# Third feed-forward of a four-layer kernel: expert outputs stored by plain indirect DMA to a table of two rows per token, both tables read back and added to x

## The chip, the cores and the metric

One core of one Trainium2 chip runs the kernel. The metric is device time in microseconds. The kernel before was run three times: 4308.01, 4302.86 and 4307.19 us, median 4307.19.

## The reference

`x` holds 64 sequences of 128 tokens of width 128. Four layers follow, each a cross attention to `ctx` and a feed-forward; every one adds to `x`. The third feed-forward, where nearly all of the change lies, is a mixture of experts with capacity: 8 experts with 512 hidden units, two experts per token, at most 2048 tokens per expert. Cut to what matters:

```python
h = layernorm(x)                                  # 8192 tokens of width 128
first, second = two best experts of softmax(h @ wg)
slot = number of earlier choices of that expert   # all first choices, then all second ones
weight = gate where slot < 2048, else 0           # a choice over capacity is dropped
y[e] = gelu(rows[e] @ w1[e] + b1[e]) @ w2[e] + b2[e]
x = x + weight_1 * y[first, slot_1] + weight_2 * y[second, slot_2]
```

The first feed-forward (another kind of expert layer, "proto") is touched as well, because tables in DRAM are filled there ahead of time.

## The kernel before

`x` stays in SBUF in 64 blocks of 128 tokens, one token per partition. The program is a row of phases; each ends in a barrier of all engines, so no phase starts before the one before it has ended on every engine.

The third feed-forward is `dispatched_experts_phase`. The routing ahead of it gives each token's two choices a row number in the DRAM table `dispatched` (8 experts x 2048 rows, 130 floats each: 128 of the normalized token, its weight, and an integer that says where the output goes). A choice that is dropped gets a spare row behind the table. The phase then has three parts.

1. The scatter. GpSimd (POOL) issues 2 x 64 indirect DMAs (L1935), one for each choice and block of 128 tokens. The weight column of `X.rows` is written by VectorE (DVE) between the two passes, once the first pass has landed (L1996, L1998). The integer column holds the token's number and is written once (L1928). SyncE (SP) meanwhile stores all of `x` to the DRAM table `summed` (L1961).
2. The tiles. The table is worked off in 32 tiles of 512 rows, four tiles per expert, in an order written out by hand for each engine. For tile t: SP loads it into `XR[t % 4]` (L1958) after the output stores of tile t-4 have landed, since these read the same buffer's indices; PE transposes it (`rows_turn`, L2060) into `f_px`, which it does for tile t+1 right behind the first unit of tile t; four hidden units of 128 follow, each with three passes up (`f_pu`) and three passes down (`f_py`), the down passes two units behind; DVE and ScalarE (ACT) split operands and apply gelu (L2022, L1981, L1985); ACT adds the bias (`f_ys`, L2028), PE transposes back (`f_po`, L2088) behind the last unit of the next tile, ACT scales by the weight into `YO[t % 2]` (L2035), and POOL issues four indirect DMAs of 128 rows that add into `summed` (L1945, `compute_op=ALU.add`). ACT writes `YO` only when the stores of tile t-2 have landed. At each fourth tile POOL waits for the landing of the four tiles before, so that two experts never add to the same row at once.
3. The return. When all stores have landed, SP loads `summed` back into `x` in eight parts of 512 KB (L1968), and DVE takes the statistics of each block for the next layernorm (L2008).

Rows of `dispatched` that no token takes must be harmless: in the first feed-forward POOL clears a tile `f_empty` (L1332), writes numbers of spare rows into its integer column (L1334), and SP stores it eight times over the table (L1323). POOL's first copies of the gates, `f_gs` (L1340), stand behind these; PE's first matmul (`f_pt`, L1470) waits for these copies and for a split of the bias by DVE (L1375, L1377).

Of the kernel before, what the change touches and what calls it, by code (L numbers as in the profile page):

```python
# [13 lines left out]
F32 = mybir.dt.float32  # L14
# [3 lines left out]
I32 = mybir.dt.int32  # L18
ALU = mybir.AluOpType
# [3 lines left out]
P = 128  # L23
# [1229 lines left out]
def gated_rows_phase(nc, R, I, name, kind):  # L1253
# [14 lines left out]
    with ExitStack() as stack:  # L1268
# [34 lines left out]
        func = ACT.Copy if kind == "proto" else ACT.Gelu  # L1303
        GBL = BL - UNG
        if kind == "proto":
            empty = sb(n_("empty"), [P, 16, ROW])
            empty_ready, table_empty = sem(n_("empty_ready")), sem(n_("table_empty"))

        def lagged(g, c, par, first, lag, f):

# [5 lines left out]
        with nc.Block() as block:  # L1316
            if kind == "proto":
                @block.sync
                def _(sp):
                    sp.wait_ge(empty_ready, 2)  # L1320
                    table = R.dispatched[0:E2 * CAP, :].rearrange("(i p r) w -> i p r w", p=P, r=16)
                    for i in range(E2 * CAP // (16 * P)):
                        sp.dma_start(table[i], empty[:]).then_inc(table_empty, 16)  # L1323
                    sp.wait_ge(table_empty, 16 * (E2 * CAP // (16 * P)))

            @block.gpsimd
            def _(pool):
                pool.wait_ge(Z["split"], 5)
                if TERMS > 3:
                    pool.wait_ge(Z["zeroed"], 1)  # L1330
                if kind == "proto":
                    nc.gpsimd.memset(empty[:], 0.0).then_inc(empty_ready, 1)  # L1332
                    pool.wait_ge(empty_ready, 1)
                    nc.gpsimd.iota(empty[:].bitcast(I32)[:, :, D + 1], [[1, 16]], base=NB * P,  # L1334
                                   channel_multiplier=16).then_inc(empty_ready, 1)

                def stage(g, par):
                    at_least(pool, Z["gt_psum"], g - 1)
                    src = g3[:, bass.ds(g * GB, GB), :, :].rearrange("p b t e -> p b (t e)")
# [529 lines left out]
def dispatched_experts_phase(nc, R, I, name):  # L1869
# [12 lines left out]
    with ExitStack() as stack:  # L1882
# [24 lines left out]
        PX = [ps(n_(f"px{i}"), [P, TR]) for i in range(2)]  # L1907
        PO = [ps(n_(f"po{i}"), [P, 4, D]) for i in range(2)]
        spare_ready, index, placed = sem(n_("spare_ready")), sem(n_("index")), sem(n_("placed"))
        ids_ready, weighted, x_kept = sem(n_("ids_ready")), sem(n_("weighted")), sem(n_("x_kept"))  # L1910
        xr_in, x_in = [sem(n_(f"xr_in{i}")) for i in range(4)], [sem(n_(f"x_in{i}")) for i in range(PARTS)]
        Z = {s: sem(n_(s)) for s in ("px_ready", "xh_ready", "xl_ready", "up_ready", "a_ready", "hi_ready", "lo_ready",
                                     "dn_ready", "ys_ready", "po_ready", "yo_ready")}
        tile_of = lambda rows, t: rows[t * TR:(t + 1) * TR, :].rearrange("(p r) d -> p r d", r=4)

        def adds(t):

            return 64 * (t // 4 + 1)

# [4 lines left out]
        with nc.Block() as block:  # L1924
            @block.gpsimd
            def _(pool):
                nc.gpsimd.iota(spare_i[:], [[NB * P, 2], [P, NB]], base=E * CAP, channel_multiplier=1).then_inc(spare_ready, 1)
                nc.gpsimd.iota(X.rows[:].bitcast(I32)[:, :, D + 1], [[P, NB]], base=0,  # L1928
                               channel_multiplier=1).then_inc(ids_ready, 1)
                pool.wait_ge(ids_ready, 1)  # L1930
                pool.wait_ge(placed, 1)
                for i in range(2):
                    pool.wait_ge(weighted, i + 1)
                    for b in range(NB):
                        nc.gpsimd.indirect_dma_start(  # L1935
                            out=R.dispatched[:, :], out_offset=bass.IndirectOffsetOnAxis(ap=place[:, i, b:b + 1], axis=0),
                            in_=X.rows[:, b, :], in_offset=None).then_inc(R.scattered, 16)
                pool.wait_ge(x_kept, 16 * PARTS)
                for t in range(NT):
                    pool.wait_ge(Z["yo_ready"], t + 1)  # L1940
                    if t % (NT // E) == 0:
                        for before in range(max(0, t - 4), t):
                            pool.wait_ge(R.added[before % 4], adds(before))
                    for j in range(4):
                        nc.gpsimd.indirect_dma_start(  # L1945
                            out=R.summed[:, :],
                            out_offset=bass.IndirectOffsetOnAxis(ap=XR[t % 4][:].bitcast(I32)[:, j, D + 1:D + 2], axis=0),
                            in_=YO[t % 2][:, j, :], in_offset=None, compute_op=ALU.add).then_inc(R.added[t % 4], 16)

            @block.sync  # L1950
            def _(sp):
                view = R.summed[0:NB * P, :].rearrange("(b t) d -> t b d", t=P)
                part = lambda i: slice(i * NB // PARTS, (i + 1) * NB // PARTS)

                def load(t):
                    if t >= 4:
                        sp.wait_ge(R.added[t % 4], adds(t - 4))
                    sp.dma_start(XR[t % 4][:], tile_of(R.dispatched, t)).then_inc(xr_in[t % 4], 16)  # L1958

                for i in range(PARTS):  # L1960
                    sp.dma_start(view[:, part(i), :], R.x[:, part(i), :]).then_inc(x_kept, 16)  # L1961
                sp.wait_ge(R.scattered, 16 * 2 * NB)
                for t in range(NT):
                    load(t)
                for t in range(NT - 4, NT):
                    sp.wait_ge(R.added[t % 4], adds(t))
                for i in range(PARTS):
                    sp.dma_start(R.x[:, part(i), :], view[:, part(i), :]).then_inc(x_in[i], 16)  # L1968

            @block.vector  # L1970
            def _(dve):
                v = nc.vector

                def split_low(t):
                    dve.wait_ge(Z["xh_ready"], t + 1)
                    v.tensor_tensor(XL[t % 2][:], PX[t % 2][:], XH[t % 2][:].bitcast(F32), ALU.subtract).then_inc(Z["xl_ready"], 1)

                def high(n):
# [12 lines left out]
                v.tensor_tensor(X.kept[:], X.kept[:], spare[:], ALU.mult).then_inc(index, 1)  # L1991
                v.tensor_tensor(spare[:], spare[:], X.slots[:], ALU.add).then_inc(index, 1)
                dve.wait_ge(index, 3)
                v.tensor_tensor(place[:], spare[:], X.kept[:], ALU.subtract).then_inc(placed, 1)
                dve.wait_ge(ids_ready, 1)
                v.tensor_copy(X.rows[:, :, D], X.weight[:, 0, :]).then_inc(weighted, 1)  # L1996
                dve.wait_ge(R.scattered, 16 * NB)
                v.tensor_copy(X.rows[:, :, D], X.weight[:, 1, :]).then_inc(weighted, 1)  # L1998
                split_low(0)
                for n in range(N):  # L2000
                    high(n)
                    low(n)
                    if n % HB == 2 and n // HB + 1 < NT:
                        split_low(n // HB + 1)
                for b in range(NB):
                    if b % (NB // PARTS) == 0:
                        dve.wait_ge(x_in[b // (NB // PARTS)], 16)
                    v.bn_stats(R.stats[:, b, :], R.x[:, b, :]).then_inc(R.stats_done, 1)  # L2008

            @block.scalar  # L2010
            def _(act):
# [18 lines left out]
                def outs(t):  # L2030
                    act.wait_ge(Z["po_ready"], t + 1)
                    if t >= 2:
                        act.wait_ge(R.added[(t - 2) % 4], adds(t - 2))
                    for j in range(4):
                        last = a.activation(YO[t % 2][:, j, :], PO[t % 2][:, j, :], ACT.Identity,  # L2035
                                            scale=XR[t % 4][:, j, D:D + 1])
# [69 lines left out]
def build(nc, I, out):  # L2106
    with ExitStack() as stack:
# [7 lines left out]
        R.ones_bf = sb("ones_bf", [P, P], BF16)  # L2115
        R.stats_done = sem("stats_done")
        R.dispatched = nc.dram_tensor("dispatched", [E2 * CAP + 2 * NB * P, ROW], F32).ap()
        R.summed = nc.dram_tensor("summed", [NB * P + SPARE, D], F32).ap()
        R.scattered = sem("scattered")
        R.added = [sem(f"added{i}") for i in range(4)]  # L2120
# [109 lines left out]
```

## Time and profile before

| | us |
|---|---|
| median of three runs | 4307.19 |
| lowest and highest | 4302.86, 4308.01 |
| the profiled execution | 4304.42 |
| its span from first to last instruction | 4302.6 |
| third feed-forward: from the first scatter to the end of the last statistics | 1996.6 to 2538.5 |
| of it the tiles, first load to last store | 2164.2 to 2518.4 |

The profile comes from one execution. Its durations are that execution's; PE is the matmul stream, PEld the weight loads beside it. An engine that issues a DMA is busy only as long as the issue takes; POOL's indirect DMAs are work of POOL, because it makes the descriptors. `A <- B` behind a wait says which instruction ended it, as far as the profile can tell. The column PEclk in the table by stretches is the granted TensorE clock as a share of 2.4 GHz.

### The profile page before, as it was taken

What the parts mean: (1) busy time and instruction counts of PE and PEld (TensorE: products, weight loads), DVE (VectorE), ACT (ScalarE), POOL (GpSimd) and SP (SyncE); (2) the same over time, 40 slices, a digit from 0 to 9 for tenths busy, and PEclk for the clock granted to TensorE, in tenths of its full rate; (3) what the DMA queues carried; (4) which work ended last, traced back from release to release, by engine and by line L of the source; (5) the groups of instructions that cost most, each with busy time, mean ns of one, the idle gap of its engine ahead of it and who ended that gap; (6) DMA issues with size and microseconds to landing.
All of it is one profiled execution on the core that took longest, in us unless ns stands there. A gap on an engine that the chain in (4) does not pass through costs nothing. (4 is left out here: it accounts for less than half of the span.)

```text
span 4302.6 us, 95379 instructions
## 1 busy us (share of the span) xinstructions
PE 3552.4 (83%) x31830; PEld 2474.5 (58%) x31831; DVE 3327.7 (77%) x6125; ACT 2333.0 (54%) x4244; POOL 1642.7 (38%) x909
## 2 busy tenths in 40 slices
PE   6983979999598899982067749999499998799999
PEld 3552646667365566662045536666366666677777
DVE  7888879997897888883044458888788778788888
ACT  3432657775475566640044436767566665466665
POOL 2210045552000545433745555555155443222222
PEclk9985989997799999985588869999699999799999
DMA  1012022222000222212123342222222112100000
GB/s 62 16 35 96 0 63 63 66 63 68 1 0 11 66 56 59 56 62 61 51 48 50 50 89 60 60 59 57 58 54 53 46 46 67 40 15 15 15 15 15
DMA packets 172168, 200.65 MB, mean 47 GB/s; under 512 B 37692, under 2 KB 126080, under 8 KB 169793
## 3 DMA queue, kind: packets, MB, share of 16 engines
q1 hardware_dynamic: 149441, 181.01, 15.7%
q0 software_dynamic: 22528, 16.92, 2.9%
q8 instruction: 132, 2.16, 0.2%
q14 instruction: 67, 0.55, 0.0%
HBM read 48.90 MB, written 38.01 MB: 20 GB/s over the span
## 5 line engine op out<-in xcount | busy, mean ns | idle before, releaser
L704 ACT ACTIVATE a_p<-a_p 128x480 f32<-128x480 f32 x832 | 501.6, 603 | 517.4 <-DVE a_p L552 515.1
L348 POOL TENSOR_TENSOR a_km<-a_k,a_slots 96x1920 fp32r<-96x1920 f32 x186 | 631.8, 3417 | 179.9 <-DMA a_k<-a_kh 179.9
L547 DVE TENSOR_REDUCE a_mx<-a_sc 128x4 f32<-128x480 f32 (+1 forms) x832 | 542.2, 652 | 126.2 <-PE a_sc L792 96.5
L552 DVE TENSOR_TENSOR a_p<-a_sc,a_mx 128x480 f32<-128x480 f32 x832 | 531.2, 638 | 18.8
L710 ACT ACTIVATE a_pt<-a_tp 120x512 f32<-120x512 f32 x832 | 487.8, 586 | 82.9 <-PE a_tp L801 77.8
L801 PE MATMUL a_tp<-ident,a_p 128*120 128x128 f32 x3328 | 510.0, 276 | 4.1 <-ACT a_p L704 2.3
L801 PEld LDWEIGHTS a_tp<-ident,a_p 128*120 128x120 f32 x3328 | 400.0, 138 | 90.0 <-ACT a_p L704 27.1
L786 PE MATMUL a_sc<-a_km,a_qr 96*128 96x480 f32 x768 | 395.8, 515 | 33.6 <-DMA a_qr<-a_ql 29.5
L825 PE MATMUL a_nd<-a_pt,a_vm 120*32 120x128 f32 x6656 | 354.5, 285 | 0.0
L825 PE MATMUL a_nd<-a_pt,a_dm 120*32 120x128 f32 x6656 | 334.4, 273 | 0.0
L1760 ACT ACTIVATE f_s<-f_pu 128x512 f32<-128x512 f32 x256 | 153.5, 600 | 212.8 <-PE f_pv L1249 212.8
L1945 POOL DMA_INDIRECT summed<-f_yo,f_xr x128 | 202.5, 1582 | 153.2 <-ACT f_yo L2035 118.8
L547 DVE TENSOR_REDUCE s_mx<-s_sc 128x4 f32<-128x512 f32 x256 | 176.3, 689 | 97.4 <-PE s_sc L792 96.7
L2060 PE MATMUL f_px<-ident,f_xr 128*128 128x128 f32 x128 | 27.4, 353 | 271.5 <-DMA f_xr<-dispatched 271.5
L560 DVE RECIPROCAL a_rd<-a_nd 128x128 f32<-128x128 f32 x256 | 242.4, 947 | 6.7 <-PE a_nd L825 6.5
L348 POOL TENSOR_TENSOR s_km<-s_k,s_slots 96x2048 fp32r<-96x2048 f32 x62 | 224.0, 3633 | 52.2 <-DMA s_k<-s_kh 52.2
L1646 POOL TENSOR_TENSOR f_ya<-f_ya,f_yg 128x512 f32<-128x512 f32 x96 | 125.1, 1303 | 302.4 <-DVE f_yg L1696 302.3
L704 ACT ACTIVATE s_p<-s_p 128x512 f32<-128x512 f32 x256 | 161.1, 629 | 146.1 <-DVE s_p L552 144.6
L1671 DVE TENSOR_TENSOR f_a<-f_s,f_pv 128x512 f32<-128x512 f32 x256 | 175.2, 684 | 76.5 <-ACT f_s L1760 68.7
L1683 DVE TENSOR_TENSOR f_al<-f_a,f_ah 128x512 fp32r<-128x512 f32 x256 | 229.0, 895 | 0.0
L786 PEld LDWEIGHTS a_sc<-a_km,a_qr 96*128 96x128 f32 x768 | 146.4, 191 | 138.3 <-issue 130.1
L825 PEld LDWEIGHTS a_nd<-a_pt,a_vm 120*32 120x32 f32 x6656 | 131.2, 108 | 141.6 <-issue 132.2
(426 smaller groups left out, 8983.4 us busy)
## 6 DMA issues: line engine op xcount, KB each, us to landing
a_qr<-a_qh SPq DMA_DIRECT2D x384, 64.0 KB, 2.0
a_k<-a_kh SPq DMA_DIRECT2D x384, 60.0 KB, 2.0
a_ctx<-in_ctxT SPq DMA_DIRECT2D x64, 240.0 KB, 2.7
a_qr<-a_ql SPq DMA_DIRECT2D x192, 64.0 KB, 2.0
a_k<-a_kl SPq DMA_DIRECT2D x192, 60.0 KB, 2.0
dispatched<-f_empty SPq DMA_DIRECT2D x8, 1040.0 KB, 12.2
f_xr<-dispatched SPq DMA_DIRECT2D x32, 260.0 KB
s_k<-s_kh SPq DMA_DIRECT2D x128, 64.0 KB, 2.0
```

What stands on the lines that cost most here:

```text
L348: v.tensor_tensor(KM[par][:, i, :, :].rearrange("p b (j k) -> p b j k", k=KN), K3[:, i, :, :].unsqueeze(2).to_broadcast([TR, GB, 4, KN]), ...
L547: v.tensor_reduce(mx[:], view, AX.X, ALU.max).then_inc(mx_ready, 1)
L552: v.tensor_tensor(PR[s % 4][:].rearrange("p (h k) -> p h k", k=k), view, mx[:].unsqueeze(2).to_broadcast([P, heads, k]), ALU.subtract).the ...
L560: v.reciprocal(RD[:], ND[bt % 2][:, 1, :]).then_inc(rd_ready, 1)
L704: a.activation(PR[s % 4][:], PR[s % 4][:], ACT.Exp).then_inc(exp_ready, 1)
L710: a.activation(PT[s % 4][0:KN, :], TP[s % 2][0:KN, :], ACT.Copy).then_inc(pt_ready, 1)
L786: last = t.matmul(SC[s % 2][:, 0:W], queries, keys, start=True, stop=not masked)
L801: last = t.transpose(TP[s % 2][0:KN, q * P:(q + 1) * P], PR[s % 4][:, q * KN:(q + 1) * KN], R.ident[:])
L825: last = t.matmul(ND[j % 2][32 * q:32 * q + 32, what, :], w, PT[s % 4][0:KN, q * P:(q + 1) * P], start=(what == 0 and i == 0), stop=(i == ...
L1671: v.tensor_tensor(A[s % 2][:], S[s % 2][:], PV[s % 2][:], ALU.mult).then_inc(Z["a_ready"], 1)
L1683: v.tensor_tensor(AL[s % 4][:], A[s % 2][:], AH[s % 4][:].bitcast(F32), ALU.subtract).then_inc(Z["lo_ready"], 1)
L1945: nc.gpsimd.indirect_dma_start(out=R.summed[:, :], out_offset=bass.IndirectOffsetOnAxis(ap=XR[t % 4][:].bitcast(I32)[:, j, D + 1:D + 2], a ...
```

## The change

The table `summed` (one row per token) becomes `chosen`, with one row per token for its first choice and one for its second, and spare rows behind. The integer column of a dispatched row says which of the two halves, so POOL writes it anew between the two passes of the scatter. No two stores now have the same target row, and they are plain. `x` stays in SBUF and is no longer stored; at the end SP loads both halves part by part into two buffers `YB`, and DVE adds them to `x`, taking the statistics of the part before in between. POOL's wait at each fourth tile goes. Since rows of dropped choices are never written, `chosen` is filled with zeros in the first feed-forward: a second memset on POOL ahead of the one of `f_empty`, and eight more stores of 1 MB on SP. The semaphores `added` are renamed `returned`.

```diff
@@ first feed-forward @@
                 def _(sp):
+                    sp.wait_ge(none_ready, 1)
+                    chosen = R.chosen[0:2 * NB * P, :].rearrange("(i p r) d -> i p (r d)", p=P, r=16)
+                    for i in range(2 * NB // 16):
+                        sp.dma_start(chosen[i], none[:]).then_inc(chosen_zero, 16)
                     sp.wait_ge(empty_ready, 2)
...
+                    sp.wait_ge(chosen_zero, 16 * (2 * NB // 16))
...
+                    nc.gpsimd.memset(none[:], 0.0).then_inc(none_ready, 1)
                     nc.gpsimd.memset(empty[:], 0.0).then_inc(empty_ready, 1)
                     pool.wait_ge(empty_ready, 1)
-                    nc.gpsimd.iota(empty[:].bitcast(I32)[:, :, D + 1], [[1, 16]], base=NB * P,
+                    nc.gpsimd.iota(empty[:].bitcast(I32)[:, :, D + 1], [[1, 16]], base=2 * NB * P,
@@ third feed-forward, POOL @@
-                nc.gpsimd.iota(X.rows[:].bitcast(I32)[:, :, D + 1], [[P, NB]], base=0,
-                               channel_multiplier=1).then_inc(ids_ready, 1)
-                pool.wait_ge(ids_ready, 1)
                 pool.wait_ge(placed, 1)
                 for i in range(2):
+                    at_least(pool, R.scattered, 16 * NB * i)
+                    nc.gpsimd.iota(X.rows[:].bitcast(I32)[:, :, D + 1], [[P, NB]], base=i * NB * P,
+                                   channel_multiplier=1).then_inc(ids_ready, 1)
+                    pool.wait_ge(ids_ready, i + 1)
                     pool.wait_ge(weighted, i + 1)
...
-                pool.wait_ge(x_kept, 16 * PARTS)
                 for t in range(NT):
                     pool.wait_ge(Z["yo_ready"], t + 1)
-                    if t % (NT // E) == 0:
-                        for before in range(max(0, t - 4), t):
-                            pool.wait_ge(R.added[before % 4], adds(before))
                     for j in range(4):
                         nc.gpsimd.indirect_dma_start(
-                            out=R.summed[:, :],
+                            out=R.chosen[:, :],
...
-                            in_=YO[t % 2][:, j, :], in_offset=None, compute_op=ALU.add).then_inc(R.added[t % 4], 16)
+                            in_=YO[t % 2][:, j, :], in_offset=None).then_inc(R.returned[t % 4], 16)
@@ third feed-forward, SP @@
-                for i in range(PARTS):
-                    sp.dma_start(view[:, part(i), :], R.x[:, part(i), :]).then_inc(x_kept, 16)
...
                 for i in range(PARTS):
-                    sp.dma_start(R.x[:, part(i), :], view[:, part(i), :]).then_inc(x_in[i], 16)
+                    at_least(sp, x_added, i - 1)
+                    for k in range(2):
+                        sp.dma_start(YB[i % 2][:, k, :, :], choice[k][:, part(i), :]).then_inc(y_in[i % 2], 16)
@@ third feed-forward, DVE @@
-                for b in range(NB):
-                    if b % (NB // PARTS) == 0:
-                        dve.wait_ge(x_in[b // (NB // PARTS)], 16)
-                    v.bn_stats(R.stats[:, b, :], R.x[:, b, :]).then_inc(R.stats_done, 1)
+                def statistics(i):
+                    dve.wait_ge(x_added, i + 1)
+                    for b in range(i * NB // PARTS, (i + 1) * NB // PARTS):
+                        v.bn_stats(R.stats[:, b, :], R.x[:, b, :]).then_inc(R.stats_done, 1)
+
+                for i in range(PARTS):
+                    dve.wait_ge(y_in[i % 2], 32 * (i // 2 + 1))
+                    x = R.x[:, part(i), :]
+                    v.tensor_tensor(x, x, YB[i % 2][:, 0, :, :], ALU.add).then_inc(first_added, 1)
+                    dve.wait_ge(first_added, i + 1)
+                    v.tensor_tensor(x, x, YB[i % 2][:, 1, :, :], ALU.add).then_inc(x_added, 1)
+                    if i > 0:
+                        statistics(i - 1)
+                statistics(PARTS - 1)
```

## Rows read from the trace of the kernel before

**Rows 1.** The page, part 1: busy us, share of the span, instructions.

```profile
PE 3552.4 (83%) x31830; PEld 2474.5 (58%) x31831; DVE 3327.7 (77%) x6125; ACT 2333.0 (54%) x4244; POOL 1642.7 (38%) x909
```

**Rows 2.** Waits, 2164 to 2560: who for whom: us, times, longest.

```profile
PE f_px L2060 <- DMA f_xr<-dispatched: 271.5, 15, 191.5
...
POOL summed L1945 <- ACT f_yo L2035: 118.8, 15, 25.0
```

**Rows 3.** Stretch, tile 4 to 30: length; PE, PEld, DVE, ACT, POOL busy; PEclk; DMA, GB/s.

```profile
2199.90:2479.03 279.13, 202.21 (x833) 157.31 (x833) 130.53 (x234) 126.93 (x260) 164.25 (x105) 0.84 0.37 50
```

**Rows 4.** Timeline of one turn: start, duration, instruction, [idle before <- releaser].

```profile
2328.59 1.12 PE L2060 MATMUL f_px<-ident,f_xr 128*128 128x128 f32 x4 [5.56 <-DMA f_xr<-dispatched]
...
2336.61 1.14 ACT L2035 ACTIVATE f_yo<-f_po,f_xr 128x128 f32<-128x128 f32 x4 [0.45 <-PE f_po L2088]
...
2338.03 1.56 POOL L1945 DMA_INDIRECT summed<-f_yo,f_xr  x1 [6.63 <-ACT f_yo L2035]
...
2343.78 1.56 POOL L1945 DMA_INDIRECT summed<-f_yo,f_xr  x1 [0.30 <-issue]
...
2347.11 0.32 SPq L1958 DMA_DIRECT2D f_xr<-dispatched  x1
...
2350.13 1.11 PE L2060 MATMUL f_px<-ident,f_xr 128*128 128x128 f32 x4 [5.67 <-DMA f_xr<-dispatched]
```

**Rows 5.** Groups on POOL, scatter and tiles: count, busy us, mean ns, idle before.

```profile
L1935 POOL DMA_INDIRECT dispatched<-f_rows,f_place x128 | 122.9, 960 | 45.2 <-issue 43.2 <-DVE f_rows L1996 2.0
...
L1945 POOL DMA_INDIRECT summed<-f_yo,f_xr x128 | 202.5, 1582 | 153.2 <-ACT f_yo L2035 118.8 <-issue 34.1 <-DMA summed<-f_yo,f_xr 0.3
```

**Rows 6.** Timeline of the scatter: ends of its two passes, first tile's load.

```profile
2071.32 0.96 POOL L1935 DMA_INDIRECT dispatched<-f_rows,f_place  x1 [0.30 <-issue]
...
2076.37 0.95 POOL L1935 DMA_INDIRECT dispatched<-f_rows,f_place  x1 [0.30 <-issue]
...
2161.67 0.95 POOL L1935 DMA_INDIRECT dispatched<-f_rows,f_place  x1 [0.30 <-issue]
2164.19 1.90 SPq L1958 DMA_DIRECT2D f_xr<-dispatched  x4
```

**Rows 7.** Stretch behind a stall (columns as rows 3), and PE's timeline behind two others.

```profile
2328.60:2332.90 4.30, 4.30 (x12) 3.56 (x13) 0.00 (x0) 0.59 (x2) 2.50 (x2) 0.50 0.42 39
...
3201.16 0.79 PE L786 MATMUL s_sc<-s_km,s_qr 96*128 96x512 f32 x1 [3.34 <-issue]
...
2176.01 0.50 PE L1245 MATMUL f_pu<-f_xh,f_w1hi 128*128 128x512 f32 x1 [1.59 <-ACT f_a L2022]
```

**Rows 8.** Timeline of the last outputs and the return; time to landing of its loads.

```profile
2500.16 1.14 ACT L2035 ACTIVATE f_yo<-f_po,f_xr 128x128 f32<-128x128 f32 x4 [0.44 <-PE f_po L2088]
...
2505.22 1.14 ACT L2035 ACTIVATE f_yo<-f_po,f_xr 128x128 f32<-128x128 f32 x4 [2.97 <-DMA summed<-f_yo,f_xr]
...
2516.82 1.55 POOL L1945 DMA_INDIRECT summed<-f_yo,f_xr  x1 [0.30 <-issue]
...
2520.19 11.16 SPq L1968 DMA_DIRECT2D x<-summed  x8
...
2524.33 1.64 DVE L2008 BATCH_NORM_STATS2 stats<-x 128x6 f32<-128x128 f32 x8 [23.42 <-DMA x<-summed]
...
2535.17 3.31 DVE L2008 BATCH_NORM_STATS2 stats<-x 128x6 f32<-128x128 f32 x16 [0.16 <-DMA x<-summed]
...
DMA to landing us min/median/max: 4.1/7.2/7.8
```

**Rows 9.** Timeline of the first feed-forward's start.

```profile
394.90 2.29 DVE L1365 TENSOR_TENSOR f_rest<-f_gates,f_g 128x2048 f32<-128x2048 f32 x1
...
402.10 1.84 POOL L1332 MEMSET f_empty<- 128x2080 f32 x1 [85.97 <-DVE f_g L1371]
...
402.53 1.49 DVE L1375 CAST f_bias<-f_bias 96x128 bf16<-96x128 f32 x1
...
405.35 0.66 PE L1470 MATMUL f_pt<-ident_bf,f_gs 128*96 128x128 bf16 x4 [67.01 <-DVE f_bias L1377]
```

More of the change, by code:

```diff
@@ L1305, in gated_rows_phase @@
         if kind == "proto":
-            empty = sb(n_("empty"), [P, 16, ROW])
+            empty, none = sb(n_("empty"), [P, 16, ROW]), sb(n_("none"), [P, 16 * D])
             empty_ready, table_empty = sem(n_("empty_ready")), sem(n_("table_empty"))
+            none_ready, chosen_zero = sem(n_("none_ready")), sem(n_("chosen_zero"))
         def lagged(g, c, par, first, lag, f):
@@ L1909, in dispatched_experts_phase @@
         spare_ready, index, placed = sem(n_("spare_ready")), sem(n_("index")), sem(n_("placed"))
-        ids_ready, weighted, x_kept = sem(n_("ids_ready")), sem(n_("weighted")), sem(n_("x_kept"))
-        xr_in, x_in = [sem(n_(f"xr_in{i}")) for i in range(4)], [sem(n_(f"x_in{i}")) for i in range(PARTS)]
+        YB = [sb(n_(f"yb{i}"), [P, 2, NB // PARTS, D]) for i in range(2)]
+        ids_ready, weighted = sem(n_("ids_ready")), sem(n_("weighted"))
+        first_added, x_added = sem(n_("first_added")), sem(n_("x_added"))
+        xr_in, y_in = [sem(n_(f"xr_in{i}")) for i in range(4)], [sem(n_(f"y_in{i}")) for i in range(2)]
         Z = {s: sem(n_(s)) for s in ("px_ready", "xh_ready", "xl_ready", "up_ready", "a_ready", "hi_ready", "lo_ready",
@@ L1914, in dispatched_experts_phase, with part, rows_back @@
         tile_of = lambda rows, t: rows[t * TR:(t + 1) * TR, :].rearrange("(p r) d -> p r d", r=4)
-        def adds(t):
+        def part(i):
+            return slice(i * NB // PARTS, (i + 1) * NB // PARTS)
+        def rows_back(t):
             return 64 * (t // 4 + 1)
@@ L1937, in _ @@
                             in_=X.rows[:, b, :], in_offset=None).then_inc(R.scattered, 16)
-                pool.wait_ge(x_kept, 16 * PARTS)
                 for t in range(NT):
                     pool.wait_ge(Z["yo_ready"], t + 1)
-                    if t % (NT // E) == 0:
-                        for before in range(max(0, t - 4), t):
-                            pool.wait_ge(R.added[before % 4], adds(before))
                     for j in range(4):
                         nc.gpsimd.indirect_dma_start(
-                            out=R.summed[:, :],
+                            out=R.chosen[:, :],
                             out_offset=bass.IndirectOffsetOnAxis(ap=XR[t % 4][:].bitcast(I32)[:, j, D + 1:D + 2], axis=0),
-                            in_=YO[t % 2][:, j, :], in_offset=None, compute_op=ALU.add).then_inc(R.added[t % 4], 16)
+                            in_=YO[t % 2][:, j, :], in_offset=None).then_inc(R.returned[t % 4], 16)
             @block.sync
             def _(sp):
-                view = R.summed[0:NB * P, :].rearrange("(b t) d -> t b d", t=P)
-                part = lambda i: slice(i * NB // PARTS, (i + 1) * NB // PARTS)
+                choice = [R.chosen[k * NB * P:(k + 1) * NB * P, :].rearrange("(b t) d -> t b d", t=P) for k in range(2)]
                 def load(t):
                     if t >= 4:
-                        sp.wait_ge(R.added[t % 4], adds(t - 4))
+                        sp.wait_ge(R.returned[t % 4], rows_back(t - 4))
                     sp.dma_start(XR[t % 4][:], tile_of(R.dispatched, t)).then_inc(xr_in[t % 4], 16)
-                for i in range(PARTS):
-                    sp.dma_start(view[:, part(i), :], R.x[:, part(i), :]).then_inc(x_kept, 16)
                 sp.wait_ge(R.scattered, 16 * 2 * NB)
@@ L1965, in _ @@
                 for t in range(NT - 4, NT):
-                    sp.wait_ge(R.added[t % 4], adds(t))
+                    sp.wait_ge(R.returned[t % 4], rows_back(t))
                 for i in range(PARTS):
-                    sp.dma_start(R.x[:, part(i), :], view[:, part(i), :]).then_inc(x_in[i], 16)
+                    at_least(sp, x_added, i - 1)
+                    for k in range(2):
+                        sp.dma_start(YB[i % 2][:, k, :, :], choice[k][:, part(i), :]).then_inc(y_in[i % 2], 16)
             @block.vector
@@ L1994, in _ @@
                 v.tensor_tensor(place[:], spare[:], X.kept[:], ALU.subtract).then_inc(placed, 1)
-                dve.wait_ge(ids_ready, 1)
                 v.tensor_copy(X.rows[:, :, D], X.weight[:, 0, :]).then_inc(weighted, 1)
@@ L2032, in outs @@
                     if t >= 2:
-                        act.wait_ge(R.added[(t - 2) % 4], adds(t - 2))
+                        act.wait_ge(R.returned[(t - 2) % 4], rows_back(t - 2))
                     for j in range(4):
@@ L2117, in build @@
         R.dispatched = nc.dram_tensor("dispatched", [E2 * CAP + 2 * NB * P, ROW], F32).ap()
-        R.summed = nc.dram_tensor("summed", [NB * P + SPARE, D], F32).ap()
+        R.chosen = nc.dram_tensor("chosen", [2 * NB * P + SPARE, D], F32).ap()
         R.scattered = sem("scattered")
-        R.added = [sem(f"added{i}") for i in range(4)]
+        R.returned = [sem(f"returned{i}") for i in range(4)]
         load_phase(nc, R, I)
```

## The prediction

> **What bounds the kernel now.** I read three things in order. First the page: PE is busy for 83% of the span and POOL for 38% [rows 1], so a change on POOL counts only where POOL is what the others wait for. Then the waits of the third feed-forward, 2164 to 2560 us. There PE's largest wait is for a load of dispatched rows, and POOL's largest is for ACT's scaled outputs [rows 2]. The first wait is 271.5 us in 15 pieces, but one piece of 191.5 us is the routing and the scatter ahead of the tiles; the other 14 are 80 us, 5.7 us each. PE waits for a load, the load waits for POOL's adding stores, and POOL waits for outputs that PE has not made: a loop. Third, the timeline of one turn of this loop [rows 4].
>
> The loop runs like this. PE turns the rows of tile t+4 early in tile t+3. Its buffer XR is that of tile t, so the load waits until tile t's four stores have landed. From tile 16's turn at 2328.59, PE, DVE and ACT need 9.16 us until ACT has finished tile 14's outputs at 2337.75. POOL starts 0.28 later and spends 7.31 on four adding stores, 2338.03 to 2345.34. 1.77 us later, at 2347.11, SP issues tile 18's load. 3.02 later PE starts it at 2350.13. The sum is 9.16 + 0.28 + 7.31 + 1.77 + 3.02 = 21.54 us, which is the whole distance 2328.59 to 2350.13. It covers two tiles: tile 15's stores run behind tile 14's, and the next odd load is in time. PE's last matmul of the turn ends at 2344.46, so PE is idle for 5.67 of the 21.54. Over 13 turns, 279.13 us [rows 3], a turn takes 21.47. So nothing here is PE-bound; the loop is latency, and POOL's four stores are a third of it.
>
> **The stores: removed and added.** One adding indirect DMA holds POOL 1.58 us on average, a plain one of the dispatch 0.96, both 128 of 128 rows [rows 5]. With the gap between instructions a plain one comes every 1.26 us (2071.32 to 2076.37 are four steps [rows 6]), so four take 3 x 1.26 + 0.95 = 4.73 in place of 7.31. The trace has no plain store of 512-byte rows from YO with indices in XR; its nearest row is the dispatch, with 520-byte rows and indices in another tile, and I take it. Bounds: 4.73 as above, 7.31 if the 1.58 is not due to the adding. From the last plain issue to what waits for its landing the trace has 2161.67 + 0.95 = 2162.62 to 2164.19, so 1.57 [rows 6], against 1.77 for the adding one. Saved per turn: 2.58 + 0.20 = 2.78. There are 14 stalls of PE, and each turn keeps a stall (5.67 - 2.78 = 2.9), so the loop still sets the pace and all of it counts: 14 x 2.78 = 38.9 us.
>
> What is late next in a turn: tile 19's load. Its tile 15 outputs are made 6.8 us after tile 14's, its stores then take 4.73 + 1.57 + 3.02 behind them, 0.3 us of waiting included about 16.4 us after tile 14's outputs; PE wants it 9.6 us after them to restart on tile 18 and some 8.4 later, so 18.0. It is in time by 1.6 us. POOL's own load falls from 15 to 10 us per turn of 18.8.
>
> The landing time was weighed against a rule. The Trainium skill, Perfetto Trace Analysis, in its account of the lifecycle of a DMA, says that the semaphore update waits until the write is confirmed and that this can take surprisingly long when the target is HBM. That speaks against any gain from a plain store, which still writes HBM; the row agrees in that 1.57 us remain. By the rule alone the landing would gain nothing, 36.1 in place of 38.9.
>
> **The clock.** After a stall of 5.56 us the granted clock is 0.50 (1.2 GHz) for 4.3 us of matmuls, then 1.00 (2.4 GHz) [rows 7]. The 4.3 us would be half as long at the upper level, so each fall costs 2.15 us, inside the 9.16. With a stall of 2.9 us it may not fall. The nearest rows: behind a stall of 3.34 us the first matmul of 512 columns took 0.79, the lower level (all six stalls of 3.3 to 3.7 us ended so), behind one of 1.59 it took 0.50, the upper one [rows 7] (of 13 stalls near 1.5 us, 3 were followed by a fall within 3 us). 2.9 is nearer to the former. I take 10 falls in 14, so 4 x 2.15 = 8.6 us gained; bounds 0 and 14 x 2.15 = 30.
>
> **The end of the tiles.** The last 16 stores ran without a break, and the last ended at 2518.37 [rows 8]. ACT's last outputs waited 2.97 us for a landing. With stores of 1.26 us POOL is up to date again after each tile; only the last two tiles, whose outputs come quickly one after the other, still queue: tile 30's outputs end at 2501.30, and eight issues from about 2501.6 end at 2511.4, so 7.0 earlier, and 0.2 for the landing: 7.2 us. Bounds: 2.4 (the last tile's four alone, 4 x 0.6) and 9.8 (16 x 0.61). The removed wait at every fourth tile costs nothing today: it falls where POOL waits for ACT anyway, and this is the cover.
>
> **x comes back: the price.** Before, eight DMAs of 512 KB, issued from 2520.19; the first landed after 4.14, six more follow 1.81 us apart (2524.33 to 2535.17), and the last statistics end at 2538.48 [rows 8]: 18.3 us, set by the transfer. After, 16 such DMAs, at most two parts (four DMAs) under way, and two adds of 128 x 1024 per part on DVE. An add over 2048 columns took 2.29 [rows 9], so one over 1024 takes about 1.22, if a fixed 0.15 is in it; two and their link 2.5. Eight statistics take 1.64. I followed the parts one by one: parts 0 and 1 land 5.9 and 9.5 us after the first issue. Part 2's loads go out when part 0 is added (8.5), part 3's when part 1 is (12.1), and so on; two loads need 2.2 + 2 x 1.8 us when the queue has run dry. DVE adds (2.5), then takes the statistics of the part before (1.6). This gives a part every 4.2 to 4.3 us, DVE and the round through SP nearly equal; part 7 is added at 38.4, and 16 statistics end at 41.7. That is 23.4 more than 18.3; with some slack at SP I take 24. From below: transfer alone, 2.3 + 16 x 1.81 + 2.5 + 3.3 = 37.1, so 18.8 more. From above: each pair of parts pays the median landing of 7.2 [rows 8], a second DMA's 1.8, the adds' 2.5 and 0.3: 11.8 for two parts, 47 + 3.3 = 50.5, so 32 more.
>
> **The start of the stage.** The eight stores of x to the old table vanish; they lay beside the scatter, whose pace does not depend on them, so nothing is gained. POOL now writes the ids after waiting for placed, and a second time after the first pass has landed: two short iotas of 64 columns with a semaphore each, 0.3 us each and 0.6 together. Behind each wait the scatter's issues are queued, and for them SP's loads and PE. From above each costs no more than the 2080-column memset, 1.84 [rows 9].
>
> **The first feed-forward.** POOL gets a second memset, 2048 columns, ahead of the old one, which took 1.84, and its first copies of the gates stand behind both. During it a DVE cast in the chain of the bias took 1.49, while PE stood waiting for this chain (405.35) [rows 9]. So the start of PE moves by one memset less what slack there is: 1.9 us, bounds 0 and 3.7. The 8 MB of zeros go out beside matmuls, on an SP that has nothing else in that stage, which lasts until about 600 us; cover is ample, and without it they would cost about 20 us.
>
> **Sum.** -38.9 - 8.6 - 7.2 + 24 + 0.6 + 1.9 = -28.2 us. The profiled execution took 4304.42 us (span 4302.6 and 1.8 around it), so 4276.2; it lies 2.8 below the median of the runs, 4307.19, and the forecast on that footing is 4279.
>
> **Rivals.** *The clock stays up.* If 2.9 us are short enough at all 14 turns, 30 us are gained in place of 8.6, and the time is 4258. For it: 10 of 13 stalls near 1.5 us left the clock alone. Against: all six of 3.3 to 3.7 brought it down. Chance 0.22. The Trainium skill, TensorE: Matmul & The Clock Gate, section on HAM oscillation, describes this pattern, a DMA wait per tile that makes every tile start cold, and would have it vanish once waits are short.
>
> *The return is latency.* Every pair of parts pays the upper bound: +32 in place of +24, and few turns keep the clock. Then -38.9 - 3 - 7.2 + 32 + 2.5 = -14.6, 4293. For it: two buffers only, and SP, DVE and queue hand over in a circle. Against: the queue holds four DMAs, not one. Chance 0.15.
>
> *Slower: the plain store holds POOL as long as the adding one.* Then the loop keeps its 21.5 us, and only the prices stay: +24 + 2.5 less 14 x 0.2, so 4331. The place is POOL's issue in the tile loop; it decides from about 1.2 us per store on: 14 turns of four and some 11 at the end make 67 stores on the path, and 26.5 / 67 = 0.4 below the 1.58. For it: source rows and index stride differ from the dispatch. Against: both index columns lie with one value per partition, and 128 dispatch issues all took 0.96. Chance 0.08.
>
> **Chances and range.** My forecast 0.52, the rivals 0.22, 0.15, 0.08, and 0.03 for something else. The range 4254 to 4300 takes in the first three cases and leaves about 0.15 out. About 0.2%, 8.6 us, is what a measurement of this kernel can tell from no change. Faster by more: the forecast and the clock rival whole and most of the latency rival, 0.86. Within: 0.05. Slower: 0.09.
>
> **What would show it.** In the trace after: plain stores near 0.96 us on POOL; turns of 18.8 us (16.6 where the clock stays at 1.00), with PE's stalls near 2.9; the last store some 55 us earlier relative to the first load; 16 loads back into x, 16 adds of 1.2 us, and 41 to 43 us from the first of these loads to the last statistics; f_pt's first matmul about 1.9 us later. It would be wrong if stores stayed at 1.5 us, if PE's stalls did not shrink, or if a part took 6 us to come back.

## The result and the profile after

The kernel after takes 4260.7 us (median of four runs, 4258.77 to 4265.72), the kernel before 4305.72 in the runs beside it. The ratio is 0.9898, with a 95% interval of 0.988 to 0.9915: 45 us faster. Forecast was 28 us of gain, 4279, with a range of 4254 to 4300. One execution of the kernel before, run beside four of the experiments, took 8560.5 us, twice the time of all others, and is left out of their ratios.

The page, part 1, of the kernel after (as [rows 1]):

```profile
PE 3539.6 (83%) x31830; PEld 2463.6 (58%) x31831; DVE 3346.6 (79%) x6141; ACT 2332.4 (55%) x4244; POOL 1570.1 (37%) x911
```

The waits of the stage (as [rows 2]), the stretch from tile 4's transposes to tile 30's (as [rows 3]), and POOL's stores (as [rows 5]):

```profile
PE f_px L2078 <- DMA f_xr<-dispatched: 226.1, 15, 192.2
...
POOL chosen L1955 <- ACT f_yo L2053: 130.5, 31, 22.2
...
2193.55:2418.76 225.21, 190.48 (x832) 147.25 (x833) 129.94 (x234) 126.95 (x260) 103.69 (x105) 0.93 0.21 62
...
L1955 POOL DMA_INDIRECT chosen<-f_yo,f_xr x128 | 127.7, 998 | 160.3 <-ACT f_yo L2053 130.5 <-issue 29.8
```

PE still waits for the loads 14 times, now 33.9 us in all (226.1 less the 192.2 ahead of the tiles) in place of 80. POOL now waits for ACT at nearly every tile, 31 times, where before it waited at every second: it has become idle in between. 13 turns take 225.21 us, 17.3 each, in place of 21.5. The granted clock of the stretch rose from 0.84 to 0.93.

One turn (as [rows 4]), timeline of the kernel after:

```profile
2295.51 1.12 PE L2078 MATMUL f_px<-ident,f_xr 128*128 128x128 f32 x4 [2.39 <-DMA f_xr<-dispatched]
...
2303.03 1.14 ACT L2053 ACTIVATE f_yo<-f_po,f_xr 128x128 f32<-128x128 f32 x4 [0.45 <-PE f_po L2106]
...
2304.45 0.96 POOL L1955 DMA_INDIRECT chosen<-f_yo,f_xr  x1 [6.06 <-ACT f_yo L2053]
...
2308.37 0.96 POOL L1955 DMA_INDIRECT chosen<-f_yo,f_xr  x1 [0.30 <-issue]
...
2310.61 0.32 SPq L1967 DMA_DIRECT2D f_xr<-dispatched  x1
...
2313.17 0.66 PE L2078 MATMUL f_px<-ident,f_xr 128*128 128x128 f32 x4 [2.29 <-DMA f_xr<-dispatched]
```

The loop is the same, each link shorter: PE's restart to ACT's outputs, 2295.51 to 2304.17, 8.66; POOL starts 0.28 later; four stores 4.88 (2304.45 to 2309.33); landing 1.28; load 2.56. The sum is 17.66, the distance of the two restarts. Means over the 14 turns, from the same timelines of both kernels:

| us per turn | before | after | saved | x 14 | forecast |
|---|---|---|---|---|---|
| PE's restart to ACT's outputs | 9.10 | 8.19 | 0.91 | 12.7 | 8.6 |
| outputs to POOL's start | 0.31 | 0.27 | 0.04 | 0.6 | 0 |
| four stores | 7.33 | 4.91 | 2.42 | 33.9 | 36.1 |
| landing to SP's load | 1.77 | 1.35 | 0.42 | 5.9 | 2.8 |
| load to PE's restart | 3.02 | 2.63 | 0.39 | 5.5 | 0 |

The return, timeline and landing of the kernel after (as [rows 8]):

```profile
2451.92 30.45 SPq L1977 DMA_DIRECT2D f_yb<-chosen  x16
...
2457.95 1.23 DVE L2021 TENSOR_TENSOR x<-x,f_yb 128x1024 f32<-128x1024 f32 x1 [17.89 <-DMA f_yb<-chosen]
2459.20 1.22 DVE L2023 TENSOR_TENSOR x<-x,f_yb 128x1024 f32<-128x1024 f32 x1
...
2466.25 1.22 DVE L2021 TENSOR_TENSOR x<-x,f_yb 128x1024 f32<-128x1024 f32 x1 [0.79 <-DMA f_yb<-chosen]
...
2487.41 1.22 DVE L2021 TENSOR_TENSOR x<-x,f_yb 128x1024 f32<-128x1024 f32 x1
...
2489.81 3.19 DVE L2016 BATCH_NORM_STATS2 stats<-x 128x6 f32<-128x128 f32 x16
...
DMA to landing us min/median/max: 4.0/5.4/7.2
```

From the first load at 2451.92 to the end of the last statistics at 2493.0 are 41.1 us, in place of 18.3: 22.8 more.

The account of the 44.4 us between the two profiled executions (4304.42 and 4260.05): the tiles, first load to last store's end, went from 354.2 to 286.4 (-67.8); last store to first load back -0.4; the return +22.8; the scatter +0.9; PE's first matmul in the first feed-forward +1.45; the stages behind the return +1.1; the rest, -2.4, lies between that matmul and the scatter, in stages that the change doesn't touch.

### The profile page after: what moved, and what is told of

The parts are those of the page before. It is cut to its first block and busy times, and to the rows that moved or that the text cites. A ratio compares the mean times of both kernels' runs of the same rounds, so it can differ in the third digit from the quotient of the medians.

```text
span 4258.2 us, 95393 instructions
## 1 busy us (share of the span) xinstructions
PE 3539.6 (83%) x31830; PEld 2463.6 (58%) x31831; DVE 3346.6 (79%) x6141; ACT 2332.4 (55%) x4244; POOL 1570.1 (37%) x911
## 3 DMA queue, kind: packets, MB, share of 16 engines
q0 software_dynamic: 8192, 16.92, 1.2%
## 5 line engine op out<-in xcount | busy, mean ns | idle before, releaser
L552 DVE TENSOR_TENSOR a_p<-a_sc,a_mx 128x480 f32<-128x480 f32 x832 | 531.4, 639 | 18.8
L2078 PE MATMUL f_px<-ident,f_xr 128*128 128x128 f32 x128 | 25.0, 328 | 226.1 <-DMA f_xr<-dispatched 226.1
L825 PEld LDWEIGHTS a_nd<-a_pt,a_dm 120*32 120x32 f32 x6656 | 199.1, 110 | 0.0
```

The source lines that it names most:

```text
L552: v.tensor_tensor(PR[s % 4][:].rearrange("p (h k) -> p h k", k=k), view, mx[:].unsqueeze(2).to_broadcast([P, heads, k]), ALU.subtract).the ...
L825: last = t.matmul(ND[j % 2][32 * q:32 * q + 32, what, :], w, PT[s % 4][0:KN, q * P:(q + 1) * P], start=(what == 0 and i == 0), stop=(i == ...
```

## The experiments

All are against the kernel after (4260.7) unless said otherwise. The theory is the loop: a turn is the sum of its five links, and a link counts as long as PE stalls.

**e1_add: the adding alone, put back.**

```diff
-                            in_=YO[t % 2][:, j, :], in_offset=None).then_inc(R.returned[t % 4], 16)
+                            in_=YO[t % 2][:, j, :], in_offset=None, compute_op=ALU.add).then_inc(R.returned[t % 4], 16)
```

> The kernel after with one word put back: its stores into the zeroed table add again, so the result is the same. Everything else of the change stays (no wait at each fourth tile, no store of x, two tables read back). Loop theory: the gain comes from what a store costs between tile t's outputs and tile t+4's load. POOL's four stores take 7.3 us again in place of 4.9, the landing 1.8 in place of 1.3 and the load 3.0 in place of 2.6, a turn 21.4 us in place of 17.3, the tiles 354 us from the first load to the last store's end in place of 286; the return stays at 41. Time 4261 + 67 = about 4328, slower than the kernel before by 0.5%. Rival (the removed waits at every fourth tile, or the removed stores of x, brought the gain): turns stay near 17.3 us and the time near 4261.

Measured: 4330.68 us, ratio to the kernel before 1.006 (1.0042 to 1.0078). Stretch of the tiles, and the waits:

```profile
2162.23:2516.16 353.93, 247.92 (x1024) 192.78 (x1024) 160.72 (x288) 157.67 (x321) 203.62 (x128) 0.83 0.36 48
...
PE f_px L2078 <- DMA f_xr<-dispatched: 272.8, 15, 191.8
...
L1955 POOL DMA_INDIRECT chosen<-f_yo,f_xr x128 | 203.6, 1591 | 151.7 <-ACT f_yo L2053 117.3 <-issue 34.4
```

All five links are those of the kernel before again (9.18, 0.27, 7.39, 1.76, 3.07). So the whole gain in the tiles is the adding's, the shorter landing and load and the clock included; what the change does otherwise costs 26 us against the kernel before.

**e6_waits_back: the other waits and stores that the change removed, put back.**

```diff
+                pool.wait_ge(x_kept, 16 * PARTS)
                 for t in range(NT):
                     pool.wait_ge(Z["yo_ready"], t + 1)
+                    if t % (NT // E) == 0:
+                        for before in range(max(0, t - 4), t):
+                            pool.wait_ge(R.returned[before % 4], rows_back(before))
...
+                for i in range(PARTS):
+                    sp.dma_start(kept_rows[:, part(i), :], R.x[:, part(i), :]).then_inc(x_kept, 16)
```

> The kernel after with what the change removed beside the adding put back: the eight stores of x to DRAM ahead of the tiles (into a tensor that nobody reads), POOL's wait for them, and its wait at every fourth tile for the landing of the four before. Theory (these cost nothing, as they lie beside the scatter and where POOL waits for ACT anyway): turns of 17.3 us, time within 3 us of 4261. Rival (they were part of the gain): some 1.3 us of landing at 8 of the tiles and the stores' time beside the scatter, 10 us or more, 4271 and above.

Measured: 4263.31 us, 0.9898 (0.9881 to 0.9914) of the kernel before, the ratio that the kernel after has. The time lies within the 3 us that the theory allowed, and the rival of 10 us is out. The profiled execution was the slowest of the four (4269.45 us, the others 4258.12 to 4264.82): it had 12 falls of the clock in its turns against 9, its turns took 17.9 us, not the 17.3 expected, and its tiles 296.2. Its stalls are not longer (226.0 us with the 191.6 ahead of the tiles), and PE's work at the lower clock level grew from 35.3 to 51.9 us, half of which is 8 of the 10 us. So the difference is mostly the clock's. About 2 us more lie in the first tiles: tile 0's outputs came 22.4 us after the first load, against 20.3 in the kernel after and 22.7 in the kernel before. No run shows why.

```profile
2162.82:2459.06 296.24, 242.30 (x1024) 187.12 (x1024) 160.06 (x288) 157.58 (x321) 126.97 (x128) 0.89 0.19 58
...
PE f_px L2086 <- DMA f_xr<-dispatched: 226.0, 15, 191.6
```

**e2_ring6 and e9_ring5: the loop opened.** Six buffers, then five, for the dispatched rows.

```diff
-        XR = [sb(n_(f"xr{i}"), [P, 4, ROW]) for i in range(4)]
+        XR = [sb(n_(f"xr{i}"), [P, 4, ROW]) for i in range(6)]
...
-                    if t >= 4:
-                        sp.wait_ge(R.returned[t % 4], rows_back(t - 4))
+                    if t >= 6:
+                        sp.wait_ge(R.returned[t % 6], rows_back(t - 6))
```

> The kernel after with six buffers for dispatched rows in place of four. Loop theory: the load of tile t+6 no longer waits for stores that have not landed, PE's 14 stalls (33.9 us) go and with them the falls of the clock; two tiles take what PE, ACT and DVE need, 13.7 us in place of 17.3. Tiles 286 - 13 x 3.6 = about 240 us, time about 4214 to 4218. Rival (another bound, POOL's stores or the loads' bandwidth, lies just behind): a turn of 16 us or more, 4245 or above.

> The kernel after with five buffers for dispatched rows. Loop theory: the demand on a store's landing moves back by one tile, 6.8 us, and the stalls are 2.3 to 2.9 us each, so one more buffer removes them all, as two did: time about 4210, 2 to 7 us of it from the clock. Rival (six buffers gained by more than the stalls, for example by letting the loads run far ahead): less than half of the 51 us, 4235 or above.

Measured: 4209.94 us (0.9786, 0.9768 to 0.9803, of the kernel before) with six, 4208.26 (0.9778, 0.9762 to 0.9794) with five. PE's wait for the loads and a stretch of the tiles, first of six, then of five buffers:

```profile
PE f_px L2078 <- DMA f_xr<-dispatched: 192.1, 1, 192.1
...
2200.00:2380.00 180.00, 176.79 (x844) 140.12 (x843) 132.13 (x238) 128.99 (x265) 104.63 (x107) 1.00 0.26 75
...
PE f_px L2078 <- DMA f_xr<-dispatched: 191.9, 1, 191.9
...
2200.00:2380.00 180.00, 175.84 (x848) 141.02 (x847) 132.84 (x239) 130.65 (x265) 106.43 (x107) 1.00 0.26 77
```

No stall is left but the one ahead of the tiles, the clock stays at its upper level, and PE is busy 98% of the stretch, at 6.8 us per tile. One more buffer is as good as two, as the sizes say: it gives a store one tile more, 6.8 us, and the stalls were 2.2 to 2.9. What is left of the loop after the change is thus worth another 50 us. With six buffers the tiles went from 286.4 to 235.6 us, 50.8 less: 33.9 are the stalls, and PE's work at the lower clock level fell from 35.3 to 6.0 us, half of which is 14.7. So the clock's share is about 15 us, not the 2 to 7 of the expectation; the total of that expectation came out all the same.

**e3_before_ring6 and e8_add_ring6: the same with adding stores.** The first is the kernel before with six buffers; the second is the kernel after with six and this line.

```diff
-                            in_=YO[t % 2][:, j, :], in_offset=None).then_inc(R.returned[t % 6], 16)
+                            in_=YO[t % 2][:, j, :], in_offset=None, compute_op=ALU.add).then_inc(R.returned[t % 6], 16)
```

> The kernel before, adding stores and all, with six buffers in place of four. Loop theory: the loop of PE, POOL and SP opens, and the next bound is POOL: four adding stores take 7.5 us per tile against 6.8 for PE, and at every fourth tile POOL waits some 2 us for landings. Tiles 20 + 32 x 7.5 + 14 = about 270 us in place of 354, time 4306 - 84 = about 4222: the change's plain stores would then be worth next to nothing, since its return costs 23 us more. Rival (the adding stores themselves, by their traffic or their pace on POOL, set the turn): the time stays within 15 us of 4306.

> Six buffers, the table of two rows per token, but the stores add (as in e1_add). Against the kernel after with six buffers it differs in the adding alone, against the kernel before with six in the waits at every fourth tile and in the return. Loop theory: POOL is the bound with 1.67 + 0.3 us per store, 7.9 us per tile, 253 us for 32 tiles, 21 ahead of the first: tiles about 276 us against 235.6 (plain) and 290.0 (adding, with the waits at every fourth tile); time about 4250. So plain stores are worth some 40 us there and the waits some 14. Rival (PE stays the bound at 6.8 us per tile because POOL catches up): within 5 us of 4210.

Measured: 4240.49 us (0.9854, 0.9836 to 0.9871) for the kernel before with six buffers, 4248.27 (0.9871, 0.9854 to 0.9887) for the adding into the new table. The stores of the first, what ACT waits for there, and the stores of the second:

```profile
L1945 POOL DMA_INDIRECT summed<-f_yo,f_xr x128 | 213.7, 1670 | 78.0 <-issue 36.0 <-ACT f_yo L2035 23.1 <-DMA summed<-f_yo,f_xr 19.0
...
ACT f_yo L2035 <- DMA summed<-f_yo,f_xr: 87.2, 26, 5.8
...
L1955 POOL DMA_INDIRECT chosen<-f_yo,f_xr x128 | 212.6, 1661 | 61.2 <-issue 38.7 <-ACT f_yo L2053 22.5
```

The kernel before with six buffers is 64 us faster than with four and 20 faster than the kernel after: the number of buffers alone does more than the change. The bound is then POOL, as expected, but I had it 18 us too fast. A store took 1.67 us, not 1.58, and the waits at every fourth tile, which cost 0.3 us in the kernel before, now cost 19.0: they lost their cover when POOL became the bound. The second kernel was forecast with 1.67 and at 4250 and came to 4248. So with the loop open, the tiles take 290.0 us (adding, with those waits), 272.4 (adding, without) and 235.6 (plain); plain stores are worth 37 us and the waits 18, against 22.8 for the return.

**e5_return4: a finer return.** 16 parts of half the size through four buffers of half the size, in the same memory.

```diff
+    PTS = 16
...
-        YB = [sb(n_(f"yb{i}"), [P, 2, NB // PARTS, D]) for i in range(2)]
+        YB = [sb(n_(f"yb{i}"), [P, 2, NB // PTS, D]) for i in range(4)]
...
-                    at_least(sp, x_added, i - 1)
+                    at_least(sp, x_added, i - 3)
```

> The kernel after with the return in 16 parts of half the size through four buffers of half the size, the same memory. If the 41.1 us of the return are the hand-over with two buffers (a part's loads start only when the part two before is added), it becomes the transfer's: 2.3 + 16 x 1.81 + a smaller last part, about 35 to 37 us, time 4256. Rival (DVE is the bound, 8 x 4.1 us of adds and statistics): 40 to 42 us, time within 1 us of 4261.

Measured: 4259.71 us, 0.9901 (0.9884 to 0.9919) of the kernel before, not told apart from 4260.7. In its trace the return takes 38.2 us in place of 41.1. DVE's timeline:

```profile
2455.13 0.69 DVE L2022 TENSOR_TENSOR x<-x,f_yb 128x512 f32<-128x512 f32 x1 [0.59 <-DMA f_yb<-chosen]
...
2468.45 0.69 DVE L2024 TENSOR_TENSOR x<-x,f_yb 128x512 f32<-128x512 f32 x1
2469.06 0.87 DVE L2017 BATCH_NORM_STATS2 stats<-x 128x6 f32<-128x128 f32 x4
2469.84 0.67 DVE L2022 TENSOR_TENSOR x<-x,f_yb 128x512 f32<-128x512 f32 x1
```

From 2456 on DVE does not wait once: 2.1 us per half part. The first add starts 3.9 us after the first load in place of 6.0, and DVE's waits behind it shrink from 2.8 to 0.6 us; twice as many, shorter instructions give 1.5 of that back. So the hand-over held only some 2 us, the rest is DVE: both theories were half right, and the return never gets down to the transfer.

**e4_early_memset: the memsets moved ahead of the gates' split.**

```diff
+                if kind == "proto":
+                    nc.gpsimd.memset(none[:], 0.0).then_inc(none_ready, 1)
+                    nc.gpsimd.memset(empty[:], 0.0).then_inc(empty_ready, 1)
                 pool.wait_ge(Z["split"], 5)
...
-                    nc.gpsimd.memset(none[:], 0.0).then_inc(none_ready, 1)
-                    nc.gpsimd.memset(empty[:], 0.0).then_inc(empty_ready, 1)
```

> The kernel after with both memsets of the first feed-forward issued by POOL at the start of its phase, where it stands idle for 86 us, in place of behind the split of the gates. Theory (the two memsets delay PE's first matmul there, directly and by slowing DVE's bias splits from 0.4 to 1.5 us each): the casts take 0.2 to 0.4 us again, and the span from DVE's first bias cast to PE's first f_pt matmul falls from 4.7 us (3.25 in the kernel before) to about 1.7. Worth 3 us, time about 4258, within what the runs can tell from 4261. Rival (the 16 MB of fills, not the memsets, hold the phase back): the span stays near 4.7.

Measured: 4264.36 us, 0.9901 (0.9885 to 0.9918): no gain. The stage's start in the kernel after, then in this one, by DVE, POOL and PE:

```profile
392.70 0.43 DVE L1362 CAST f_xh<-f_htall 128x512 fp32r<-128x512 f32 x1 [0.97 <-PEq L69]
...
393.78 1.22 DVE L1370 CAST f_g<-f_gates 128x2048 bf16<-128x2048 f32 x1
...
402.23 1.81 POOL L1338 MEMSET f_none<- 128x2048 f32 x1 [85.96 <-DVE f_g L1378]
...
404.48 1.49 DVE L1382 CAST f_bias<-f_bias 96x128 bf16<-96x128 f32 x1
...
406.80 0.63 PE L1477 MATMUL f_pt<-ident_bf,f_gs 128*96 128x128 bf16 x4 [68.34 <-POOL f_gs L1347]
```

```profile
390.63 1.80 POOL L1335 MEMSET f_none<- 128x2048 f32 x1 [76.40 <-POOLq L69]
...
390.67 2.04 DVE L1363 CAST f_xh<-f_htall 128x512 fp32r<-128x512 f32 x1 [0.97 <-PEq L69]
392.75 0.69 DVE L1365 TENSOR_TENSOR f_xl<-f_htall,f_xh 128x512 fp32r<-128x512 f32 x1
393.36 2.20 DVE L1371 CAST f_g<-f_gates 128x2048 bf16<-128x2048 f32 x1
...
404.77 0.66 PE L1478 MATMUL f_pt<-ident_bf,f_gs 128*96 128x128 bf16 x4 [68.34 <-DVE f_bias L1385]
```

The local forecast was right: from the first bias cast to PE's first matmul 2.1 us (402.65 to 404.77) in place of 4.7 (the kernel before has 3.4 here, 401.95 to 405.35, not 3.25). But the memsets now run beside two other casts of DVE on the same chain, which take 2.04 and 2.20 us in place of 0.43 and 1.22, and from DVE's first cast to PE's first matmul both kernels take 14.1 us. The cost moved ahead by ten microseconds and stayed. The subtraction between the casts, with two operands, took 0.69 us beside the memset and without it.

**e7_all: six buffers, the finer return and the early memsets together.** The diffs are those of e2_ring6, e5_return4 and e4_early_memset; its heads:

```diff
+        XR = [sb(n_(f"xr{i}"), [P, 4, ROW]) for i in range(6)]
+        YB = [sb(n_(f"yb{i}"), [P, 2, NB // PTS, D]) for i in range(4)]
```

> The kernel after with the three edits together: six buffers for dispatched rows, the return in 16 parts through four buffers, both memsets early. If they act in different stages, their gains add: 50.8 for the buffers, 2.8 for the return (41.1 to 38.2 us in its trace), 3 for the memsets: time about 4205, the fastest so far. If the return or the start of the first feed-forward were hidden behind something else, it stays at 4210.

Measured: 4208.53 us, 0.9773 (0.9757 to 0.9789). The return takes 38.9 us in its trace (41.3 with six buffers alone), the memsets again give nothing. It cannot be told apart from five or six buffers alone (4208.26, 4209.94); these three are the fastest, 2.1 to 2.3% below the kernel before, and the one with five buffers changes nothing but their number.

## Why the prediction was right, and where it was not

The way and the mechanism were right: the loop, its parts, and the stall that stays. The size was 28 against 44 us, inside the range. The turns were forecast at 18.8 us with stalls near 2.9 and took 17.3 with stalls of 2.2 to 2.9; the last store was to end some 55 us earlier and ended 67.8 earlier.

That the measured 4260.7 lies close to the 4258 of the rival with the clock up at every turn is a coincidence, since nine falls remained. The 16 us missing from the forecast are landing and load 8.6, the clock 4.1, the return 1.2, less 2.2 for the stores; most of the rest, some 5 us, lies in the first tiles and in stages that the change doesn't touch.

*The stores.* 36.1 forecast, 33.9 measured: the dispatch was the right row for the price of a plain store. It averaged 1.00 us in the tiles, not 0.96; some took 1.08.

*Landing and load.* 2.8 forecast, 11.4 measured; this is the step that was most mis-sized. I took the landing from the end of the scatter and left the load at 3.02 us. Both run beside the stores of the tile behind, on the same 16 DMA engines. By the DMA part of the page for 2190 to 2390, the stores' queue before and after:

```profile
q0 software_dynamic: 10915, 4.98, 29.1%
...
q0 software_dynamic: 2976, 6.10, 9.1%
```

In the same stretch the plain stores move more bytes (6.10 MB, the turns being shorter) in 2976 packets, 9.1% of the engines' time, where the adding ones needed 10915 packets and 29.1%. e1_add has 10800 packets and 28.8% there, and brings the landing and the load back to 1.76 and 3.07 by the adding alone, so they belong to it; that the packets are how is argued from these rows and was not tried apart. The Trainium skill (Perfetto Trace Analysis, lifecycle of a DMA) has the semaphore wait until the write is confirmed, which can take surprisingly long when the target is HBM. The trace agrees in that 1.35 of 1.77 us stay; that the landing would gain nothing, as I drew from it, did not come out.

*The clock.* 8.6 forecast (4 of 14 falls gone), 12.7 measured. Nine falls are left of 14, so five are gone, and the remaining ones are shorter: PE's work at the lower level (granted clock 0.50, 1.2 GHz) shrank from 63.4 to 35.3 us, half of which is 14. Stalls were 2.2 to 2.9 us long, and after nearly equal stalls the clock was down at 2295.51 (2.39 us, then four transposes in 1.12) and up at 2313.17 (2.29 us, then 0.66). The stretches behind these two restarts:

```profile
2295.50:2298.90 3.40, 3.39 (x10) 2.87 (x11) 0.00 (x0) 0.00 (x0) 2.28 (x3) 0.52 0.14 43
2313.20:2316.60 3.40, 3.40 (x17) 2.85 (x18) 0.58 (x2) 1.18 (x2) 2.35 (x3) 1.00 0.11 39
```

Between 2.2 and 2.9 us the length of the stall doesn't decide it: the shortest, 2.24 us ahead of 2227.24, was followed by the lower level too. The rival that the clock stays up at all turns was wrong at a stall of 2.3, and came true in e9_ring5 with no stall at all. Between two kernels with the same links, a turn went from 17.3 us (9 falls) to 17.9 (e6_waits_back, 12 falls), and 13 turns make that some 8 us. Such differences from one execution to the next hide small edits here.

*The odd tile's load.* Forecast was that it is in time by 1.6 us. It was, but only behind a fall of the clock, where it landed 1.3 to 2.8 us ahead of its transposes. In the five turns in which the clock stayed up it landed 0.0 to 0.1 us ahead, so with four buffers and full clock the odd tiles stand at the edge of a stall as well.

*The end of the tiles.* 7.2 forecast. ACT's outputs of tile 30 and POOL's last store, timeline of the kernel after (as [rows 8]):

```profile
2439.31 1.14 ACT L2053 ACTIVATE f_yo<-f_po,f_xr 128x128 f32<-128x128 f32 x4 [0.44 <-issue]
...
2449.59 0.96 POOL L1955 DMA_INDIRECT chosen<-f_yo,f_xr  x1 [0.30 <-issue]
```

From the end of these outputs to the last store's end are 10.1 us, and 17.1 before (2501.30 to 2518.37): 7.0 saved. With the 58.6 of the table this leaves some 2 of the 67.8 us. They lie in the first tiles: tile 0's outputs came 22.7 us after the first load before and 20.3 after, and 20.2 to 22.4 in the other runs with no edit that explains it.

*The return.* 41.7 forecast, 41.1 measured, 24 against 22.8 in the sum; an add took 1.22 us as worked out. Neither bound was met: not the transfer alone, nor the latency. That rival gave 50.5 and is out. *The start of the stage.* 0.6 against 0.9. *The first feed-forward.* 1.9 against 1.45, and 16 MB of zeros beside the matmuls cost nothing that shows. *The slower rival* (a plain store as dear as an adding one) fell with the first row of the stores; e1_add shows its price: 26 us above the kernel before, forecast 24. The 4330.68 and the 4331 agree more closely than that because the forecast started from 4307.19 and the kernel before took 4304.23 beside e1_add.

## What to carry to other kernels

When an engine's wait closes a loop over several engines, write the loop down as a sum of links that equals the distance of two restarts; every link then has its price per turn, and so has one more buffer, which here was worth more (52 us on top of the change, 64 for two of them without it) than the whole change (45). An operation that is made cheaper in such a loop can shorten the transfers beside it as well: here 11.4 us came on top of the stores' own 33.9. A wait that costs next to nothing while its engine is idle (0.3 us here) has its full price when that engine becomes the bound (19.0). A two-microsecond memset on GpSimd was not free beside VectorE's casts, in either of the two places tried on their chain.

## What the runs showed of the hardware

- An indirect DMA of 128 rows of 512 bytes holds GpSimd 1.58 us when it adds and 1.00 when it is plain, and makes 144 and 32 packets (22528 and 8192 in the queue over the whole kernel, of which 4096 are the 128 dispatches, alike in both).
- With six buffers, where POOL was the bound, an adding store took 1.67 us on average (e3_before_ring6) and 1.66 (e8_add_ring6).
- A load of 260 KB took 3.0 us from its issue to PE's start beside adding stores, and 2.6 beside plain ones.
- VectorE's casts took longer while GpSimd ran a memset (2.04 us in place of 0.43, 1.49 in place of 0.22), a subtraction of two float32 tiles of 128 x 512 did not (0.69 either way).
- A stall of 2.3 us on PE was followed by the lower clock (granted 0.52) in some turns and not in others (1.00) of the same kernel.
